# An expert layer, four selective-scan layers and an expert layer on one core: VectorE takes six of a phase's sixteen products by C in place of five

## What is computed

```python
x = x + 0.5 * ffn(layernorm(x))        # 8 experts of 128 -> 344 -> 128, silu(g) * u, best 2 of 8 by router
x = x + attn(layernorm(x))             # 4 layers of the block below, then @ Wout + bout
x = x + 0.5 * ffn(layernorm(x))

# one of the 4 layers, D_INNER = 256, D_STATE = 16, DT_RANK = 64
xn = rmsnorm(x) ; xp, z = split(xn @ Win)
xc = silu(causal_depthwise_conv(xp))               # 4 taps
dt, Bm, Cm = split(xc @ Wx)
delta = softplus(dt @ Wdt + bdt) ; A = -exp(A_log)
dA = exp(delta[:, d] * A[d, n])
h  = dA * h + (delta * xc)[:, d] * Bm[:, n]        # over the 512 tokens
y  = sum_n h * Cm[:, n] + xc * Dp
x  = x + (y * silu(z)) @ Wblk
```

## Time and profile before

| | us |
|---|---|
| median of 3 runs | 4797.47 (4790.85 to 4800.3) |
| profiled execution | 4809.85 |
| its span, first to last instruction | 4808.1 |
| busy: GpSimd, VectorE, TensorE, ScalarE | 4287.1, 4167.2, 4080.0, 3332.1 |

### The profile page before, as it was taken

The page is one execution under the profiler, slowest core; times in us unless marked ns, Lnnn a source line. Parts: engine busy times, 40 slices in busy tenths (PEclk is TensorE's granted clock), DMA queues, the critical chain, the costliest instruction groups (busy, mean ns, idle before and its releaser), DMA issues.

```text
span 4808.1 us, 49171 instructions
## 1 busy us (share of the span) xinstructions
PE 4080.0 (85%) x11584; PEld 1309.7 (27%) x11584; DVE 4167.2 (87%) x5567; ACT 3332.1 (69%) x4979; POOL 4287.1 (89%) x2281
## 2 busy tenths in 40 slices
PE   7758776899998988899899989999899989578869
PEld 2212221232232322232232322222232323122223
DVE  2559888899999999999999999999999999888853
ACT  3556666677777777777777777777777777666734
POOL 0469999999999999999999999999999999999960
PEclk9869887999999999999999999999999999688869
DMA  2224433443344334433443344334433443344310
GB/s 60 56 54 108 106 83 86 100 105 85 83 109 103 85 83 109 108 83 86 104 108 79 84 109 108 85 80 109 106 82 83 108 108 81 88 100 106 72 39 5
DMA packets 136616, 425.06 MB, mean 88 GB/s; under 512 B 15885, under 2 KB 35278, under 8 KB 135951
## 3 DMA queue, kind: packets, MB, share of 16 engines
q1 hardware_dynamic: 136335, 421.92, 37.6%
HBM read 145.04 MB, written 8.39 MB: 32 GB/s over the span
## 4 chain that ended last, share of the span: by engine, by line
PE 23%; DVE 19%; POOL 19%; issue 19%; ACT 13%; SPq 3%; DMA 3%; DVEq 0%; ACTq 0%; POOLq 0%
POOL work L821 10%; POOL work L811 8%; DVE work L642 7%; DVE dA_ps L642 6%; PE d_ps L383 4%; PE b_ps L370 4%; SPq L312 3%; ACT dA_ps L493 3%; PE a_ps L370 3%; ACT L517 2%; DMA bc_sb<-bc_rows 2%; PE y_ps L354 2%; ACT L518 2%; ACT sg_sb L517 2%; PE a_ps L376 2%
## 5 line engine op out<-in xcount | busy, mean ns | idle before, releaser
L821 POOL TENSOR_TENSOR work<-dd_sb,bc_sb 128x1024 f32<-128x1024 f32 x1024 | 2406.4, 2357 | 75.2 <-issue 38.7
L493 ACT ACTIVATE dA_ps<-dd_sb,a_sb 128x512 f32<-128x512 f32 x2048 | 1366.7, 685 | 764.5 <-DVE work L642 453.3
L642 DVE TENSOR_TENSOR_SCAN work<-dA_ps,work 128x512 f32<-128x512 f32 x1408 | 1659.8, 1207 | 42.5 <-POOL work L821 21.3
L811 POOL TENSOR_TENSOR work<-work,bc_sb 128x1024 f32<-128x1024 f32 x704 | 1660.4, 2359 | 29.5 <-DVE work L642 29.3
L383 PE MATMUL d_ps<-sg_sb,wd_sb 128*128 128x512 f32 (+1 forms) x1536 | 788.1, 649 | 41.4 <-DVE sg_sb L720 41.4
L642 DVE TENSOR_TENSOR_SCAN dA_ps<-dA_ps,work 128x512 f32<-128x512 f32 x640 | 780.5, 1220 | 36.2 <-ACT dA_ps L493 16.3
L354 PE MATMUL y_ps<-work,sel_sum 128*32 128x512 f32 x4096 | 607.8, 669 | 94.5 <-POOL work L811 60.9
L370 PE MATMUL b_ps<-xT_sb,wg_sb 128*128 128x512 f32 (+1 forms) x768 | 440.1, 656 | 66.6 <-ACT sg_sb L517 66.1
L370 PE MATMUL a_ps<-xT_sb,wg_sb 128*128 128x512 f32 (+1 forms) x768 | 440.3, 656 | 33.3 <-ACT sg_sb L517 30.6
L647 DVE TENSOR_TENSOR work<-dA_ps,bc_sb 128x512 f32<-128x512 f32 x640 | 441.4, 690 | 18.5
L376 PE MATMUL a_ps<-xs_sb,wu_sb 128*128 128x512 f32 (+1 forms) x768 | 415.7, 623 | 32.6 <-DVE sg_sb L720 24.7
(11 more groups left out here) (101 smaller groups left out, 3999.9 us busy)
## 6 DMA issues: line engine op xcount, KB each, us to landing
dd_sb<-dd_src SPq DMA_DIRECT2D x512, 512.0 KB, 8.5
bc_sb<-bc_rows SPq DMA_DIRECT2D x256, 512.0 KB, 7.5
xr_sb<-in_L_attn_x SPq DMA_DIRECT2D x16, 256.0 KB, 2.9
bc_rows<-dbc_sb SPq DMA_DIRECT2D x128, 32.0 KB, 1.7
out<-xr_sb SPq DMA_DIRECT2D x16, 256.0 KB, 6.1
wg_sb<-in_L_ffn_Wg SPq DMA_DIRECT2D x1, 1376.0 KB
wu_sb<-in_L_ffn_Wu SPq DMA_DIRECT2D x1, 1376.0 KB
wd_sb<-in_L_ffn_Wd SPq DMA_DIRECT2D x2, 512.0 KB
```

Of the source, the lines that this page charges most:

```text
L493: act.activation(dA_ps[:, g % NDA, :], dd_sb[:, b, c, 0, :], ACT.Exp, scale=a_sb[:, l, b, j, c:c + 1]).then_inc(dA_ready, 1)
L642: dve.tensor_tensor_scan(dA if on_dve(i) else tile, dA, tile, 0.0, ALU.mult, ALU.add).then_inc(scanned, 1)
L811: pool.tensor_tensor(work[:, g % RING], work[:, g % RING], bc_sb[:, j, 0, :].unsqueeze(1).broadcast_to([128, 2, T]), ALU.mult).then_inc(po ...
L821: pool.tensor_tensor(work[:, g % RING], dd_sb[:, b, 2 * (i % 2):2 * (i % 2) + 2, 1, :], bc_sb[:, j, 1, :].unsqueeze(1).broadcast_to([128, ...
```

## The change

VectorE takes the products of six halves of a phase and GpSimd of ten, where it was five and eleven. The units whose second half VectorE multiplies are 0, 2, 3 and 4, 6, 7, three in each block; they were 0, 2, 3 and 5, 6. All tables of offsets get other numbers. Nothing else differs: the same sums are made from the same products.

```diff
-CORE = {"exp": -11, "scan": -1, "dbu": -6, "dve_prod": 1, "pool_prod": 17, "sum": 29, "y0": 87, "y1": 14}
-PREP = {"sq": -22, "ms": 11, "rms": 2, "xn": 13, "xp0": 13, "conv0": 16, "xp1": 25, "conv1": 25, "silu_xc": 27, "z0": 33,
-        "zc0": 29, "z1": 45, "zc1": 41, "silu_z": 59, "wx": 37, "dbc": 34, "rows": -6, "dt0": 50, "sp0": 56, "delta0": 65,
-        "du0": 74, "dt1": 73, "sp1": 73, "delta1": 82, "du1": 117, "dd0": 22, "dd1": 50, "bc": 20}
-NEAR = {"sq": 21, "ms": 28, "rms": 30, "xn": 41, "xp0": 35, "conv0": 44, "xp1": 52, "conv1": 55, "silu_xc": 59, "z0": 63,
-        "zc0": 60, "z1": 66, "zc1": 62, "silu_z": 91, "wx": 67, "dbc": 73, "rows": 21, "dt0": 77, "sp0": 84, "delta0": 87,
-        "du0": 90, "dt1": 94, "sp1": 94, "delta1": 108, "du1": 116, "dd0": 46, "dd1": 80, "bc": 44}
-POST = {"wblk": 84, "h": 95, "attn": 98, "x2": 106}
-POST_NEAR = {"wblk": 20, "h": 22, "attn": 25, "x2": 48}
-FFN_AT = {"gb": 3, "xs": 3, "g0": 5, "g1": 8, "g2": 9, "burst": 5, "u0": 12, "u1": 12, "u2": 13, "hh0": 16, "hh1": 16,
-          "hh2": 23, "down": 27}
-START = {"load": -130, "bn": -60, "nb": -51, "xtok": -47, "xt": -47, "xT": -43, "lg": -40, "lg_sb": -39, "mx": -38,
-         "mi": -36, "gap": -27, "we": -32, "eq": -19, "den": -21, "inv": -20, "comb": -15, "ct": -20, "gates": -23}
-END = {"yt": 25, "xo": 34, "bn": 44, "nb": 58, "xtok": 48, "ht": 79, "h": 79, "store": 68, "acc": 12}
+CORE = {"exp": -8, "scan": -1, "dbu": -10, "dve_prod": 1, "pool_prod": 15, "sum": 29, "y0": 89, "y1": 16}
+PREP = {"sq": -28, "ms": 9, "rms": 9, "xn": 12, "xp0": 16, "conv0": 13, "xp1": 25, "conv1": 24, "silu_xc": 29, "z0": 32,
+        "zc0": 34, "z1": 45, "zc1": 42, "silu_z": 61, "wx": 44, "dbc": 39, "rows": 13, "dt0": 48, "sp0": 53, "delta0": 60,
+        "du0": 63, "dt1": 65, "sp1": 73, "delta1": 75, "du1": 82, "dd0": 18, "dd1": 46, "bc": 27}
+NEAR = {"sq": 24, "ms": 27, "rms": 34, "xn": 41, "xp0": 42, "conv0": 45, "xp1": 50, "conv1": 55, "silu_xc": 61, "z0": 63,
+        "zc0": 61, "z1": 65, "zc1": 64, "silu_z": 93, "wx": 73, "dbc": 76, "rows": 28, "dt0": 79, "sp0": 78, "delta0": 85,
+        "du0": 91, "dt1": 90, "sp1": 98, "delta1": 105, "du1": 104, "dd0": 55, "dd1": 89, "bc": 48}
+POST = {"wblk": 90, "h": 93, "attn": 101, "x2": 108}
+POST_NEAR = {"wblk": 18, "h": 19, "attn": 29, "x2": 29}
+FFN_AT = {"gb": 3, "xs": 3, "g0": 5, "g1": 6, "g2": 7, "burst": 7, "u0": 9, "u1": 11, "u2": 13, "hh0": 15, "hh1": 15,
+          "hh2": 21, "down": 28}
+START = {"load": -130, "bn": -60, "nb": -49, "xtok": -46, "xt": -48, "xT": -42, "lg": -41, "lg_sb": -35, "mx": -33,
+         "mi": -31, "gap": -32, "we": -27, "eq": -29, "den": -26, "inv": -29, "comb": -26, "ct": -21, "gates": -15}
+END = {"yt": 24, "xo": 30, "bn": 34, "nb": 41, "xtok": 69, "ht": 76, "h": 78, "store": 118, "acc": 13}
...
-DVE_UNITS = (0, 2, 3, 5, 6)
+DVE_UNITS = (0, 2, 3, 4, 6, 7)
 NDP, NPP = len(DVE_UNITS), HALVES - len(DVE_UNITS)
```

## The result

The changed kernel is slower: 4870.46 us median (4869.35 to 4888.19) against 4798.89; the ratio is 1.0159, 95% interval 1.0142 to 1.0175. The forecast was 4753. The profiled execution has a span of 4867.9 us, 59.8 more than before.

The account below looks back on a forecast made before the run. GpSimd, 97.5% busy in the ten cycles, was taken as the bound; gains of 12 + 14 + 9 + 7 + 2 = 44 us off the median 4797.5 gave 4753, range 4698 to 4815 (the forecast's own 4725 to 4780).

Parts of the forecast that it names:

- Outside the middle: Ramps before 943 and after 3895.1 us: GpSimd bounds them, so relieving it gains 14 + 9 + 7 + 2 us.
- Costs of the moved work: Per phase GpSimd loses 2.36 us, VectorE gains 1.46; over 64 phases 151 us relieved, 94 loaded; 0.69 us per product.
- The SyncE queue: First dd load moves ahead of first bc load and its wait; up to 25.2 us of GpSimd's dd waits can go.
- VectorE's idle time: Middle, 43 phases: VectorE becomes the bound, idle 88 us, between 75.3 and 162.8; stage 2940 us, a gain of 12.
- rival 1: VectorE keeps its waits, being TensorE's own latency: 162.8 us idle remain, 31 us slower, 4828; chance 0.18.
- The waits from the new ticks: GpSimd's ring reuse after the sum has 9 ticks, were 13: loss up to four times 10.7 us, counted in the 88.
- The bc load behind dd: SyncE's bc load has 34 ticks, 18 us, before its reader, so the loads' 8.5 + 7.5 us are hidden.
- The router's chain: Asks VectorE at tick -29 for what GpSimd does at -26: free, or up to 35 us over 32 layers; nothing taken.
- Rival 3: TensorE idles longer where a layer opens and its clock falls: 2.5 us a cycle, 27 lost; 4780; chance 0.10.
- Rival 4: Balance only: VectorE's idle time falls to about 130 us, ramps pay for the middle; no change, 4797; chance 0.12.
- Rival 2: VectorE as tight as GpSimd was, ramps at their maxima: 75 us gained, 4723; chance 0.14.
- What was asked of the profile: Signs: VectorE busiest from 943 us, GpSimd 94 to 95%, cycle about 273.5 us, VectorE's up projection waits about halved.

Follow-up runs that it names:

- e1: The changed kernel with the load of x two ticks earlier (-132 for -130), ahead of the first dd load in SyncE's queue: 4804.34 us, ratio to before 1.0013.
- e5: The kernel before with part of the computation left out, GpSimd multiplying only the first tile of each half by C: 4757.72 us, ratio 0.9912.
- e2: The kernel before with the six units 0, 2, 3, 4, 6, 7 and its own old ticks: 4863.04 us, ratio 1.0132.
- e7: The changed kernel (new ticks) with the five units of before and the load of x first: 4931.11 us, ratio to before 1.0272.
- e12: e5 with the up projections reading the unscaled x, so not waiting for broadcast and scaling: 4758.83 us.
- e8: e1 with only the last of an expert's three down matmuls made: 4914.95 us, ratio 1.0245.
- e9: The changed kernel with VectorE's batch norm statistics that open an expert layer at -53, not -60, load of x still late: 4836.65 us, ratio 1.0101.

## Why the prediction was wrong

The spans by stage, forecast and measured against before, in us:

| stage | forecast | changed kernel | e1 (load first) |
|---|---|---|---|
| to the 4th phase | -2 | -6.4 | -3.4 |
| ramp, 8 phases | -14 | -14.4 | -12.6 |
| middle, 43 phases | -12 | +90.6 | +19.4 |
| behind it | -16 | -10.0 | -8.0 |
| sum | -44 | +59.8 | -4.6 |

**Outside the middle: the sum right, its reason only in part.** 32 forecast, 30.8 measured. The ramp's 14 came as 14.4; ahead of it 6.4 for 2, behind the middle 10.0 for 16, so that the sum is this near is partly luck. The reason given for the ramp was that GpSimd bounds it, so that less work for GpSimd is a gain by itself. e5 and e2 in the same eight phases:

```profile
390.20:914.89 524.69, 401.13 (x1136) 119.78 (x1136) 471.00 (x606) 364.06 (x551) 428.68 (x269) 0.82 0.42 97
```

```profile
401.32:944.30 542.98, 407.67 (x1136) 121.80 (x1136) 485.29 (x623) 364.86 (x550) 502.56 (x261) 0.81 0.41 95
```

e5 takes 93 us from GpSimd and wins 15.4, so GpSimd is the bound for about the first 15 us only. e2 is the forecast's own exchange, 19 us less for GpSimd and 12 more for VectorE, and the ramp is 2.9 us longer, not 14 shorter. The new ticks alone don't do it either: 544.4 in e7. Only both together give 14 us, and the sum had nothing for that but GpSimd's waits for dd.

**Costs of the moved work: right.** VectorE's busy time grew by 96.9 us in e2 (4264.1 for 4167.2), 94 forecast; a product costs 0.69 there (530.2 / 768). GpSimd lost 141.6 in e2 and 144.4 in the changed kernel, 151 forecast. That the product isn't slowed by GpSimd held.

**The SyncE queue: the step that failed most, 71 us.** The part on ticks weighed what the first dd load passes in SyncE's queue, and named the first bc load and its wait. It did not name the load of x, two ticks ahead of dd before, whose offset the change leaves alone. An offset that doesn't change still changes its place when its neighbours move. The changed kernel less e1 in the middle is 90.6 - 19.4 = 71.

**VectorE's idle time: the other step that failed, 31 us.** The sum took 88 us for 43 phases between 75 and 163, because the waits were for matmuls that GpSimd's products hold up. e5 shows that they weren't: with GpSimd at 81% VectorE's idle time is 155.2 us where it was 150.7. In e2, the exchange with the old ticks, it is 139.0, not the forecast's share for 40 phases, 82. This is rival 1, given 0.18, and its price: 62.8 us over 43 phases was its term, e2 has 49.4 over 40. Its argument, many short waits like a tight chain's, was the one to weigh; the counterargument, that VectorE must wait somewhere if GpSimd is at 98%, took the highest share of busy time for the bound. e1 loses only 19.4, since the new ticks let VectorE do the same work in 41 us less of busy time in the ten cycles (2657.2 in e2, 2615.9), a gain that no step of the prediction had (10 of them at line 765).

e1's idle time is 150.7 us again, but not in the same places. In three windows of each cycle it fell with the new ticks, from 121.6 to 89.0 us in all, part of what the forecast wanted; in the third it rose from 29.2 to 61.7. By length, the third windows are 34 us longer than before and the other thirty 14 us shorter. So what e1 still loses in the ten cycles lies wholly where a layer starts and attention's output is made, the place where the clock still falls (0.95 in the third window, 0.97 on average before). The lead is the order of line 376 and the output projection told above; it wasn't run.

**The waits from the new ticks: mis-sized, on an engine that had time.** GpSimd's wait for the sum that frees its half of the ring was put at up to four times 10.7 us; it is 102.0 in the changed kernel and 62.0 in e1. The bc load behind dd was to be hidden; GpSimd waits 79.3 us for it in e1, and has no such wait in the kernel before. The router's chain, up to 35 us, holds GpSimd for 63.3. They fall on GpSimd, idle 175.9 us of e1's ten cycles; what they hand on to the others is not shown.

**The other rivals.** Rival 3, the clock, named the right place, TensorE idle where a layer starts and the clock falling with it, but not the late load that makes it large: changed kernel less e1 is 6.5 us a cycle, wait included. With the load first its price of 2.5 us a cycle is near what is left there, 3.4 us in the third window. Rival 4's number, 4797, is near e1's 4804. Rival 2 had nothing for it. What was asked of the profile: the ramp over 10 us shorter, yes; VectorE busiest, yes, with 65.4 us a phase for 66.3; line 647 at most 0.69 us, yes; a granted clock of a cycle not below 0.95, just; GpSimd at 94 to 95%, no: 91.4, in e1 93.6; a cycle of 273.5 us, no: 283.2, in e1 276.7. VectorE's waits for up projections were to be halved and were the sign against rival 1; over the ten cycles they fell from 67.6 to 42.9 us (4.3 a cycle), but the wait for the gate broadcast grew from 26.0 to 68.3 (61.9 in e1). The sign looked at one wait of a chain, and the wait had moved to the next.

**Open.** What makes up VectorE's 150 us. By the rows they are mostly waits for TensorE's up projections and broadcasts. Shown is what doesn't set their length with the old ticks: GpSimd's pace (e5), the scaling's link (e12). A shorter TensorE queue couldn't be tried without the clock falling (e8). Nor is it shown which of the new ticks cost e7 its 134 us, or why the first window of a cycle is longer in e9.

## What to carry to other kernels

The engine with the highest busy share need not be the bound: take work from it in an experiment, from its neighbour too, and see which one moves the stage; an engine at 94% with waits that nobody removes can be the bound ahead of one at 97%. Where queues are laid out by a table, compare the order of each queue line by line, DMA issues first, also for the entries that didn't change: a load that slips behind a blocked DMA cost 66 us in one kernel and 200 in the other. And price a wait by what stands behind it: 2.1 us at one engine became 6.5 us a cycle, half of it behind TensorE's longer pause, in matmuls at a lower clock. And when a total such as an engine's idle time comes out unchanged, split it by stretch: 150.7 us twice was 33 us less in three windows of a cycle and 33 more in the third.

## What the runs showed of the hardware

Less work for TensorE went with a lower clock and a longer time: with two of three down matmuls left out, 640 fewer matmul instructions in the ten cycles, the granted clock was 0.87 for 0.97, TensorE's busy time 44 us less and the stage 66 us longer than in e1.

The compare of line 765, whose two inputs lie in SBUF, took 159 to 1110 ns before. With the new ticks, in the changed kernel, it takes

```profile
L765 DVE TENSOR_TENSOR eq_sb<-iota_e,mf_sb x64: 178/184/193, 29.5 to 4780.1; 128x32 f32<-128x32 f32 x64
```

GpSimd is then waiting for VectorE's next step (line 770, 63.3 us in e1) and runs no long product beside it. The one long instance of e7, 2.32 us, starts 0.08 us behind the start of a GpSimd product of 2.34 us and ends 0.06 us behind its end. This fits the rule of the Trainium skill's page "SBUF — State Buffer", section "SBUF: two separate sides", cited above. In the prediction the rule was a risk for the new products; what it changed was this compare, a gain of some 13 us in all (22.7 us of busy time in e2, 9.2 in e1).
